# First block of a gated cross-attention and FFN kernel: the scale of the down weights taken before the cosines, its rows split from step 13

## What is computed

```
# 1. attention over a row's neighbours: cosine of ctx column t with columns t-1, t, t+1
sim  = [cos(ctx, shift_right(ctx)), cos(ctx, ctx), cos(ctx, shift_left(ctx))]
f    = layernorm(x)                       # over the 1024 columns
x1   = x + tanh(g_xattn) * sum_k W_k @ (f shifted by k-1  *  sim_k)      # W_k: 128 x 128
# 2. FFN on n = layernorm(x1)
h      = relu(n @ up_w) ** 2              # 1024 -> 2048
shared = h @ down_w                       # 2048 -> 1024
routed = (n @ fc1_w @ expert_w @ fc2_w) * sum(top2(n @ gate_w))
out  = x1 + tanh(g_ffn) * (layernorm(shared + routed) * gamma + beta)
```

## Time and profile before

| | |
|---|---|
| median of three runs | 1022.1 us |
| the profiled execution, its own time | 1020.98 us |
| its span, first to last instruction | 1019.2 us |
| TensorE matmuls, busy | 948.0 us (93%) |
| VectorE, ScalarE, GpSimd, busy | 476.0, 322.9, 344.3 us |
| mean granted TensorE clock | 0.980 |

### The profile page before, as it was taken

How to read it: one execution, slowest core, us unless ns; L and a number is a source line. 1 busy time by engine, 2 the same in 40 slices (tenths; PEclk the granted TensorE clock), 3 DMA queues, 4 the chain that set the end, 5 groups by cost and what they waited for, 6 DMA issues and landing times.

```text
span 1019.2 us, 12378 instructions
## 1 busy us (share of the span) xinstructions
PE 948.0 (93%) x4562; PEld 441.1 (43%) x4562; DVE 476.0 (47%) x840; ACT 322.9 (32%) x441; POOL 344.3 (34%) x159
## 2 busy tenths in 40 slices
PE   2888799946999999999999999999999999999996
PEld 1346544412444444444444444444444444444442
DVE  6365687757355325446755125445674222221112
ACT  2557677444133212233331112233331112211111
POOL 4340225266946151133556241133654200001110
PEclk9999999977999999999999999999999999999998
DMA  8797897312241453434133363433034333200001
GB/s 347 227 313 259 302 395 262 95 45 90 73 124 42 135 206 122 129 104 113 40 117 91 98 212 128 136 103 116 24 101 134 93 105 104 83 1 1 22 21 41
DMA packets 64000, 131.29 MB, mean 129 GB/s; under 512 B 35266, under 2 KB 35394, under 8 KB 62658
## 3 DMA queue, kind: packets, MB, share of 16 engines
q1 hardware_dynamic: 63218, 127.84, 38.2%
q10 hardware_dynamic: 720, 2.62, 0.6%
HBM read 105.09 MB, written 19.07 MB: 122 GB/s over the span
## 4 chain that ended last, share of the span: by engine, by line
PE 78%; DVE 8%; ACT 3%; issue 3%; POOL 2%; DMA 2%; DVEq 2%; POOLq 1%; ACTq 0%; SPq 0%
PE psS L1337 30%; PE psR L1287 16%; PE psS L1287 16%; PE psR L1347 8%; PE psP L1255 5%; PE psP L1268 2%; DVE ring L1066 1%; POOL big L535 1%; DVE s L908 1%; DMA sim_scratch<-simo 1%; DVE s L904 1%; DMA g_col<-in_g_ffn 1%; DVEq L875 1%; POOLq L534 1%; PE psR L1393 1%
## 5 line engine op out<-in xcount | busy, mean ns | idle before, releaser
L1337 PE MATMUL psS<-big,hid 128*128 128x512 f16 x1536 | 336.8, 381 | 6.0 <-issue 5.8
L1337 PEld LDWEIGHTS psS<-big,hid 128*128 128x128 f16 x1536 | 150.2, 98 | 188.1 <-issue 8.1
L1287 PE MATMUL psS<-xT,ring 128*128 128x512 f16 (+1 forms) x912 | 191.7, 371 | 2.4 <-DVE xT L1012 1.7
L1287 PE MATMUL psR<-xT,ring 128*128 128x512 f16 (+1 forms) x912 | 190.0, 368 | 0.0
L1287 PEld LDWEIGHTS psS<-xT,ring 128*128 128x128 f16 x912 | 89.7, 99 | 102.0 <-issue 4.2
L1287 PEld LDWEIGHTS psR<-xT,ring 128*128 128x128 f16 x912 | 89.2, 98 | 97.2
L522 POOL TENSOR_TENSOR y<-y,lgb 128x1024 f32<-128x1024 f32 x15 | 39.2, 2612 | 255.5 <-ACT y L673 255.5
L1030 DVE SCALAR_TENSOR_TENSOR y<-psR,rw,y 128x1024 f32<-128x1024 f32 x15 | 19.2, 1282 | 143.6 <-PE psR L1347 143.6
L1347 PE MATMUL psR<-w,lgb 128*128 128x512 f16 x384 | 85.5, 379 | 0.0
L493 POOL TENSOR_TENSOR sides<-scr 128x1024 f32<-128x1024 f32 x12 | 29.2, 2431 | 147.1 <-DMA scr<-in_ctx 147.1
L512 POOL TENSOR_TENSOR ring<-f_buf,ring 128x1024 f32<-128x1024 f32 x18 | 39.2, 2176 | 99.0 <-ACT f_buf L641 58.9
(11 more groups left out here) (198 smaller groups left out, 998.2 us busy)
## 6 DMA issues: line engine op xcount, KB each, us to landing
ring<-pair_scratch SPq DMA_DIRECT2D x60, 512.0 KB, 3.3
ring<-sim_scratch SPq DMA_DIRECT2D x18, 504.0 KB
big<-in_w_up SPq DMA_DIRECT2D x8, 1024.0 KB, 11.1
out_rows<-y SPq DMA_DIRECT2D x15, 512.0 KB, 3.0
hid<-in_w_down SPq DMA_DIRECT2D x14, 512.0 KB, 8.0
big<-in_w_down SPq DMA_DIRECT2D x14, 512.0 KB, 6.6
scr<-in_ctx SPq DMA_DIRECT2D x12, 576.0 KB, 4.0
pair_scratch<-ring SPq DMA_DIRECT2D x12, 512.0 KB, 7.3
```

The lines of the kernel that those rows point to most:

```text
L1287: mm = pe.matmul(up_bank[t % NR][:, cols], rows[:, a, k, :], xT[:, k, b, cols], start=(k == 0 and a == 0 and b == 0), stop=(k == KB - 1 an ...
L1337: mm = pe.matmul(psS[:, HALF * h:HALF * h + HALF], hT[:, i, a, P * j:P * j + P], dn[:, i, b, HALF * h:HALF * h + HALF], start=(i == 0 and ...
```

## The change

In the first block alone: the scale of the down weights is made in step 13 instead of 14, and before the cosines, which also move from step 14 to 13. The sums of sequences 2 and 3 of the context come in steps 9 and 12 instead of 10 and 13. The rows are split in steps 13 to 19, two to a step up to row 9 and then one (before: three to a step in steps 15 to 19); rows 12 to 15 stay for the down half (before: row 15 alone). GpSimd takes the lo of rows 1, 3, 11 and 13 instead of 1, 4, 7, 10 and 13: rows 1 and 3 before it weighs sequence 0 of the next block, row 11 behind that, row 13 behind `f_lo(1,0)`. TensorE does 12 row blocks instead of 8 before `xattn(1,0)`.

```diff
-        SUM_T, SCALE_T = 11, 14
-        DN_SPLIT = {15: (0, 3), 16: (3, 6), 17: (6, 9), 18: (9, 12), 19: (12, 15)}
-        DN_LATE = range(15, IT)
-        DN_POOL = [1, 4, 7, 10, 13]
+        SUM_T, SCALE_T = 11, 13
+        DN_SPLIT = {13: (0, 2), 14: (2, 4), 15: (4, 6), 16: (6, 8), 17: (8, 10), 18: (10, 11), 19: (11, 12)}
+        DN_LATE = range(12, IT)
+        DN_POOL = [1, 3, 11, 13]
         SIM_T = (3, 6, 9, 12)
+        SIM_FIRST = (4, 7, 9, 12)
-        XATTN_AT, XATTN_FIRST = (5, 0, 0, 0), (8, 12, 10, 6)
+        XATTN_AT, XATTN_FIRST = (5, 0, 0, 0), (12, 12, 10, 6)
 # GpSimd, up half
-                    for c in DN_POOL[0:3]:
+                    for c in DN_POOL[0:2]:
                         dn_lo(c)
                 weigh(m, 0)
                 if first:
-                    for c in DN_POOL[3:]:
-                        dn_lo(c)
+                    dn_lo(DN_POOL[2])
 # GpSimd, down half
                 f_lo(m, 0)
+                if first:
+                    dn_lo(DN_POOL[3])
 # ScalarE, up half
-                    if phase_a and t == COS_T + first:
+                    if phase_a and t == COS_T:
                         norms(m)
 # VectorE, up half
-                        if t == SIM_T[j] + first:
+                        if t == (SIM_FIRST if first else SIM_T)[j]:
                             sums(m, j)
-                    if phase_a and t == COS_T + first:
-                        cosines(m)
-                    if first and t == SUM_T:
-                        dve.wait_ge(dn_sq, IT)
-                        norm_sum(WDN, LT, LT + IT)
                     if first and t == SCALE_T:
                         norm_scale(WDN, 5)
                         ...
                         dve.drain().then_inc(scale_rdy, 1)
+                    if phase_a and t == COS_T:
+                        cosines(m)
+                    if first and t == SUM_T:
+                        dve.wait_ge(dn_sq, IT)
+                        norm_sum(WDN, LT, LT + IT)
 # TensorE, first up half
-                    if t == SCALE_T:
+                    if t == SCALE_T + 1:
                         norm_over_rows(WDN, 1, 5)
```

## The result

Eight runs of the changed kernel have a median of 1016.24 us (1014.81 to 1018.35), eight of the kernel before 1022.96 (1020.31 to 1026.17): ratio 0.9935, 95% interval 0.9918 to 0.9952. It is 6.7 us faster; 7.4 were forecast, and 1016.2 lies in the range of 1008.5 to 1019.5.

What follows compares the result with a forecast made beforehand. TensorE, 93% busy, bounds the kernel; waits and clock at the first block's down half cost 27.8 us, after the change 9.3 + 1.9 + 7.3 + 1.9 = 20.4. Gain 7.4: 1013.6, as a median 1014.7; range 1008.5 to 1019.5.

Steps and rivals of the forecast that it cites:

- lost: wait after the gates: TensorE before sequence 0's down half: starts at 211.2, 3.5 later than before, idle 9.3 us.
- lost: wait at sequence 1: TensorE at sequence 1: `take_s` ends at 250.2, behind row 15 and a chain of 14.25, so a wait of 7.3 us.
- Sums: Steps 9 to 12: context sums one step earlier cost between nothing and 2.3 us; 0.5 taken, step 13 at 177.2.
- Steps 14 to 16: VectorE: steps begin at 186.9, 193.7 and 201.5; `weigh`'s three products alternate with rows 4 to 7 from 198.3 to 206.6.
- signs of being wrong: Row 15 over 3 from 235, L1337 waiting on GpSimd's rows, `weigh(1,0)` after 202, or first block keeping its length.
- Tile 19: TensorE, up half: needs step 15's bank by about 195, just met; a miss is hidden by the wait for step 17.
- Where the stall goes: After `xattn`'s wait is gone, `take_s` is late next: TensorE waits 7.3 us at sequence 1 and loses 1.9 of clock.
- Clock: TensorE's matmuls after a wait run at lower clock: 1.9 us lost after the gates and 1.9 at sequence 1.
- Rival 2: Few collisions between GpSimd and VectorE: row 15 by 231 or sooner, gain over 11 us, 1004 to 1011; chance 0.18.
- rival 3: VectorE's steps stay at 8.1 us: slower by 2.4, 1024.5; in part or whole 1017 to 1027, chance 0.27.
- rival 4: No effect at L1255: `f_los` later than the 12 row blocks; costs nothing while `take_s` is later still; no separate chance.

Runs made afterwards that it cites:

- The late `weigh`: Changed kernel with one wait more: GpSimd starts `weigh(1,0)` only when 14 hidden tiles are done; 1016.14 us, 0.9933 of before.
- the early `take_s`: Changed kernel with ScalarE's `take_s` of sequence 0 moved ahead of `x1_normal(1,0)`, `x_hi` and `f_his(1,1)`; 1015.81 us, 0.9928 of before.
- the version with 8 row blocks: Changed kernel with 8 row blocks instead of 12 ahead of `xattn(1,0)`; 1013.3 us, 0.9911 of before; run again 1013.67 us, 0.9916.

## Why the prediction was right

The sign, the mechanism and the place of the new limit held. That the sum came so close is partly luck, as several of its terms were off and cancelled. Point by point, after less 1.97:

| | forecast | measured |
|---|---|---|
| step 13 begins | 177.2 | 179.3 |
| step 14 | 186.9 | 189.0 |
| step 16 | 201.5 | 201.3 |
| step 17 | 208.9 | 210.2 |
| step 19 | 217.6 | 218.9 |
| `f_los(1,0)` done | 228.0 | 229.1 |
| row 15 done | 234.8 | 235.7 |
| sequence 1 starts | 250.2 | 250.4 |
| lost: a tile of the up half | 0 | 1.06 |
| lost: wait after the gates | 9.3 | 9.3 |
| lost: its clock | 1.9 | 2.95 |
| lost: wait at sequence 1 | 7.3 | 5.0 |
| lost: its clock | 1.9 | 2.8 |
| lost in all (before 27.8) | 20.4 | 21.1 |
| gain | 7.4 | 6.7 |

The starts of sequence 2 (289.72 before, 285.36 less 1.97 after) give a gain of 6.3, by a slip of the prediction and small gaps that the table leaves out. The slip: 48 matmuls in one piece take 10.52 in the trace of before, not 10.36, so the clock after the gates cost 1.7 there, not 1.9:

```profile
243.97 10.52 PE L1337 MATMUL psS<-big,hid 128*128 128x512 f16 x48
```

*Sums.* Mis-sized: 0.5 taken, 2.6 measured. GpSimd's last pair of products waited for the context load until 172.35, so 170.4 (169.2 in the kernel before): the load was issued earlier but did not land earlier, and VectorE waited for the products in step 12. With the sums back in their old steps the kernel was as fast.

*Steps 14 to 16.* The 2.1 us were made up by step 16, by luck. The store of the cosines left SyncE at 188.52, so 186.6 where the prediction had 184.5, and `weigh` waited for their load until 202.19, so 200.2 where it had 198.3. (Later than 202 was one of its signs of being wrong; the time as measured is 0.2 past it.) Rows 4 and 5 were almost done by then and ran free (2.47), and only rows 6 and 7 alternated with the products: step 15 took 5.9 instead of 7.8, step 16 9.0 instead of 7.4. The late `weigh` shows that the alternation is what made a step long. The Trainium skill ("SBUF — State Buffer", "Who interferes with whom") calls the shared ports an exclusive lock, and says that issue order decides who blocks; the 6.50 us of rows 6 and 7 agree with it.

*Tile 19.* Missed its bank by 1.06, and that was hidden, as forecast.

*Where the stall goes.* Right: the early `take_s` removes it. Row 15 came 0.9 late, and the chain behind it was shorter, 13.6 us to the end of `f_his(1,1)` instead of 14.25, so that sequence 1 started within 0.2 of the forecast. The prediction held that nothing in this chain waits for TensorE work that moves. In the kernel before one instruction of it did, VectorE's use of the result of `xattn(1,0)`:

```profile
244.18 0.75 DVE L967 SCALAR_TENSOR_TENSOR work<-psP,coef,work 128x512 f32<-128x512 f32 x1 [0.55 <-PE psP L1255]
```

After the change `xattn(1,0)` is done at 237, before VectorE asks, and this wait is gone. TensorE's wait at sequence 1 is 2.3 shorter than forecast, because TensorE came later by as much: 1.3 from step 17 and 1.0 from the clock. A later TensorE and a shorter wait cancel as long as `take_s` sets the start, which is why the sum was off by less than its terms.

*Clock.* The term of 1.9, taken from one restart of before, was too small: 2.95 and 2.8 were lost.

*Rivals.* Rival 2 (few collisions) and rival 3 (steps of 8.1) did not come; the steps took 6.4, 5.9, 9.0, 4.9 and 3.8. In rival 4 I said that a late `f_los` costs nothing while `take_s` is later still; the version with 8 row blocks shows more, that a wait put there can save the clock at the next.

## What to carry to other kernels

When a wait on the bound engine is covered, look for what the next hand-over stands behind on the other engines' lists, and price that chain before counting the gain: here 27.8 us could be won, and 6.7 were. Of the 21.1 still lost, 13.3 lay at the last tile and the start of sequence 0, and 7.8 where ScalarE took a finished sum only behind three pieces of work for the next block. The 7.8 set the end: with `weigh` late the wait after the gates was 4.5 us shorter, and nothing was won. Moving the one instruction of ScalarE was worth nothing that could be told from noise until the output buffer's own chain was shortened too; both together gave as much again as the change. The same move in the kernel before made it slower, so an early place in a list is safe only where what it waits for is already there.

## What the runs showed of the hardware that was not expected

A wait of the same length does not cost the same clock. In two profiles of the changed kernel and in four variants TensorE waited 9.3 us after the gates, and the 72 matmuls behind it took 18.65 and 18.35, and 17.97, 17.94, 17.82 and 17.23, against 15.70 warm: 1.5 to 3.0 us lost. Before, after 5.75 us, it was 1.7. The granted clock stayed at half for some 6 us of unbroken matmuls in the changed kernel, from 214.49 until within 220 to 222 (mean 0.88 there, so until about 220.5). In the kernel before it was 3.5 us, from 207.69 until about 211.2:

```profile
210.00:212.00 2.00, 2.00 (x7) 0.70 0.02 4
```

Why one restart costs more than another after the same wait was not tested.
